# A mixture-of-experts kernel: the routing weights travel in the gathered rows, not in a table made by matmuls

## The chip, the cores and the metric

The kernel runs on one core of a Trainium2 chip. The metric is the device time of one execution in microseconds (us), lower is better; several executions are timed and the median is given. One further execution was taken by the hardware profiler.

## The reference

There are 2,048 tokens of 512 float32 values (4 batches of 512). The first stage multiplies each token by a dense matrix and adds a low-rank term chosen per batch; call its result `y`. The second stage is a mixture of 16 experts, of which each token uses two:

```
logits = y @ gate_w.T ; probs = softmax(logits)
topk_w, topk_idx = top_k(probs, 2) ; topk_w /= sum(topk_w) + 1e-20
g = y @ w_gate[e].T ; u = y @ w_up[e].T ; h = silu(g) * u      # 352 wide
out = x + sum over the two chosen e of topk_w * (h @ w_down[e].T)
```

## The kernel before, in words

The core has a matmul engine (TensorE, PE), two elementwise engines (VectorE, DVE, and ScalarE, ACT), GpSimd (POOL) and the engine that issues most transfers (SyncE, SP). Each runs its own list of instructions in order and waits on semaphores. `m_...` semaphores are counted up by PE, `v_...` by DVE, `a_...` by ACT, `d_...` by transfers. Every float32 product is made of three products of split values (high times high, high times low, low times high), so DVE and ACT split every operand into a high and a low part first.

**First stage.** `y` is made in 16 chunks `c` of 128 tokens: PE accumulates a chunk (`y_base`, `y_rank`), ACT copies it from its bank into `y_st` (`y_stage`), and SP stores it into the DRAM tensor `y_rows` (L395). In between, PE, ACT and DVE work out the routing: for each token its two experts, its softmax weights, and a slot for each of its two choices. Slots are sorted by expert and cut into tiles of 128 rows, all of one expert; a tile that an expert does not fill stays partly empty. There are 40 tiles in this run.

**The tables by slot.** A slot's token must be known by slot, but is computed by token. `slot_tables` (L607) does that with 32 small matmuls, one for each of the 32 pairs of chunk and choice: `oh_m` (one-hot of the place in a tile) times `oh_q` (one-hot of the tile, times the value to carry). `oh_q` has TABS = 5 values: two parts of the token's number, and the slot's weight cut into three bf16 parts (`w_part`). The first two tables are made in one pass of 32 matmuls during chunk 12 (`AT_TABLES`); the three weight tables in a second pass of 32 matmuls behind `gate_up(0)`. DVE makes the three weighted one-hots (`weigh`, L1090 and L1170), and adds up the three tables into `wtab` (L1177 to L1179). ACT scales a tile's result with its column of `wtab` in `y_weighted`.

**Second stage.** For each tile `t`, POOL gathers its 128 rows of `y_rows` into `xg` (`gather`, L1229). PE turns them over (`x_turn`, L625) for tiles below N_PE = 8. For the later ones SP copies them apart (`rows_apart`, L428) and DVE turns them (`x_turned`, L1150). ACT and DVE split the turned rows (`x_evac`, `y_low`), PE makes gate and up (`gate_up`, L693, 24 matmuls), ACT and DVE make `hh` (`silu`, L847, `product`, L1165), PE turns it (`h_turn`, L667) and makes the result (`down`, L722, 9 matmuls), ACT weighs it (`y_weighted`, L856), and POOL adds it to the output with an accumulating transfer (`scatter`, L1250). The order on each engine is written out by hand.

**The experts' weights.** An expert's weights come as two transfers, "gu" (1,408 KB) and "dn" (768 KB), into one of two raw buffers (`load_part`, L319), and ACT and DVE split them (L353, L355). The first expert's are loaded behind chunk 7's store. The second's are loaded behind chunk 15's store (`C_SECOND`). The third's are loaded by `later_weights(0)`, which SP comes to when gather 4 has landed (`N_LATE`). In this run tiles 0 to 2 belong to the first expert, 3 and 4 to the second, 5 to 7 to the third.

**The first gathers.** `gather(0)` and `gather(1)` may go before the last chunks are stored. PE turns the tokens' numbers of tiles 0 and 1 into one row (`need_turn`), DVE takes their maxima (`need`, semaphore `v_need`), and POOL waits for the stores up to these alone. `gather(2)` waits for all 16 stores, `gather(3)` for `h_turn(0)`, and `gather(4)` for `x_turn(2)`.

The lines that set this order at the beginning of the second stage, on PE:

```
gate_up(0)
e.wait_ge(v_ohq, 1)
e.wait_ge(v_need, 1)
slot_tables(bank[7], 2, TABS - 2)
words[1] = tile_word(e, 1)
h_turn(0)
gate_up(1)
x_turn(e, count, 2)
words[2] = tile_word(e, 2)
down(0)
```

Of the kernel before, what the change touches and what calls it, by code (L numbers as in the profile page):

```python
# [32 lines left out]
P = 128  # L33
# [34 lines left out]
TABS = 5  # L68
# [8 lines left out]
N_PE, NXS = 8, 4  # L77
N_LEAD, N_COPY = 9, 5
# [4 lines left out]
C_SECOND, N_LATE = CH - 1, 4  # L83
# [5 lines left out]
C_ID, C_IQ, C_TOK, C_ADP, C_AT, C_BEF, C_TOP, C_RNK, C_SEL, C_SCL, C_GT, C_IDS, CW = (  # L89
    0, P, P + TQ, *(P + TQ + CH + i for i in range(5)),  # L90
    *(P + TQ + CH + 4 + RANK + i for i in (0, P, P + 1, P + 1 + KH * NEXP, P + 1 + KH * NEXP + NBATCH)))
# [3 lines left out]
def build(nc, cst, rcst, head, head2, wt, wpt, wb, wbt, xin, x, wall, out):  # L95
    with ExitStack() as ctx:  # L96
# [7 lines left out]
        def region(start, size):  # L104
# [96 lines left out]
        late = [r_c(f"xg{i}", [P, H], F32) for i in range(N_EARLY, NXG)]  # L201
        ys = [r_c(f"ys{i}", [P, H], F32) for i in range(N_EARLY)]
        xg = [r_c(f"xg{i}", [P, H], F32) for i in range(N_EARLY)] + late
# [5 lines left out]
        w12 = r_c("w12", [P, NSEL], F32)  # L209
        w_part = [r_c(f"w_part{i}", [P, NSEL], BF16) for i in range(3)]  # L210
        w_rest = [r_c(f"w_rest{i}", [P, NSEL], F32) for i in range(2)]
        w_top = [r_c(f"w_top{i}", [P, CH], F32) for i in range(2)]
        w_sum, w_inv, w_one = [r_c(n, [P, CH], F32) for n in ("w_sum", "w_inv", "w_one")]
        tok_a, emp_f = [r_c(n, [P, TQ], F32) for n in ("tok_a", "emp_f")]
# [19 lines left out]
        y_dram = nc.dram_tensor("y_rows", [NTOK, H], F32, kind="Internal").ap()  # L234
# [19 lines left out]
        v_sh, v_cho, v_w12, v_ohq, v_ohm, v_tab, v_idx, v_w, v_gidx = [  # L254
            sem("v_" + n) for n in ("sh", "cho", "w12", "ohq", "ohm", "tab", "idx", "w", "gidx")]
# [59 lines left out]

        def load_part(e, part, ex, at):
# [42 lines left out]
        def _(e):  # L359
# [25 lines left out]
            for c in range(CH):  # L385
# [46 lines left out]
            for t in range(N_PE - N_COPY + 1):  # L432
                later_weights(t)
            for t in range(N_PE, NTILE + N_COPY):
                if t < NTILE:
                    rows_apart(t)
                if N_PE < t < NTILE - NRAW + N_COPY:
# [8 lines left out]
        def _(e):  # L446
# [169 lines left out]
            def x_turn(e, count, t):  # L616
                with in_use(e, count, t):
# [5 lines left out]
                    for k in range(KH):  # L623
                        rows = xg[t % NXG][:].rearrange("p (r k) -> p k r", k=KH)[:, k]
# [13 lines left out]
            for c in range(3, CH):  # L638
                for k in range(c == 3, KH):
# [112 lines left out]
        def _(e):  # L752
# [113 lines left out]
            split_weights(e, count, 3, ahead, "gu", a_gu)  # L866
            silu(1)
            x_evac(2)
# [31 lines left out]
        def _(e):  # L900
# [69 lines left out]
            done[0] += 4  # L970
# [37 lines left out]
            def token_weights():  # L1008
# [5 lines left out]
                e.tensor_tensor(w12[:, 0:CH], w1[:], w_one[:], ALU.mult).then_inc(v_chain, 1)  # L1014
                done[0] += 1
                step(e.tensor_tensor(w12[:, CH:NSEL], w2[:], w_one[:], ALU.mult))
                step(e.tensor_copy(w_part[0][:], w12[:]))
                step(e.tensor_tensor(w_rest[0][:], w12[:], w_part[0][:], ALU.subtract))
                step(e.tensor_copy(w_part[1][:], w_rest[0][:]))
                step(e.tensor_tensor(w_rest[1][:], w_rest[0][:], w_part[1][:], ALU.subtract))  # L1020
                e.tensor_copy(w_part[2][:], w_rest[1][:]).then_inc(v_w12, 1)
# [67 lines left out]
            def weigh(i):  # L1089
                e.tensor_tensor(oh_q[:, :, 2 + i], where, wide(w_part[i][:]), ALU.mult).then_inc(v_chain, 1)  # L1090
                done[0] += 1

            where = oh_q[:, :, 4]
# [3 lines left out]
            e.tensor_scalar(oh_q[:, :, 1], where, cs[:, C_AT:C_AT + 1], None, ALU.mult).then_inc(v_chain, 1)  # L1097
            done[0] += 1
            for k in range(TOPK):
                ks = slice(k * CH, (k + 1) * CH)  # L1100
                e.tensor_tensor(oh_q[:, ks, 0], where[:, ks], cs[:, C_TOK:C_TOK + CH].unsqueeze(2).to_broadcast([P, CH, TQ]),
                                ALU.mult).then_inc(v_chain, 1)
                done[0] += 1
            e.wait_ge(v_chain, done[0])
# [5 lines left out]
            step(e.tensor_scalar(tok_a[:], bank[4][:, 0:TQ], float(P), 0.0, ALU.subtract, ALU.max))  # L1110
            e.tensor_tensor(gidx[:], tok_a[:], bank[4][:, TQ:2 * TQ], ALU.add).then_inc(v_gidx, 1)
# [233 lines left out]
```

## Time and profile before

| | us |
|---|---|
| median of 3 executions | 348.83 (348.81 to 350.17) |
| the profiled execution, its own time | 347.8 |
| its span, first to last instruction | 346.0 |
| PE busy in the span | 335.8 (97%) |
| DVE busy | 233.8 (68%) |
| ACT busy | 179.0 (52%) |
| POOL busy | 129.7 (37%) |

The span is the stretch that the trace covers; 1.8 us of the execution's own time lie outside it. A busy share is an average over stages. What sets the end is read from the chain of work that ended last and from the idle time of the engine on it.

### The profile page before, as it was taken

How to read it: one execution, taken by the hardware profiler on the slowest of the kernel's cores; microseconds unless marked ns; L12 is line 12 of the kernel's file. 1: busy time of each engine (PE TensorE's matmuls, PEld its weight loads, DVE VectorE, ACT ScalarE, POOL GpSimd, SP SyncE). 2: the span in 40 equal slices, each digit the busy share in tenths (PEclk: the TensorE clock that was granted, in tenths of full speed). 3: DMA queues.
4: the chain of work that ended last, by engine and by line, in shares of the span. 5: the costliest groups of instructions: out<-in, count | busy, mean ns of one | idle time of the engine just before them, and what ended most of it. 6: DMA issues, size and time to landing. Idle time of an engine off the chain costs nothing.

```text
span 346.0 us, 7810 instructions
## 1 busy us (share of the span) xinstructions
PE 335.8 (97%) x1879; PEld 297.1 (86%) x1879; DVE 233.8 (68%) x307; ACT 179.0 (52%) x242; POOL 129.7 (37%) x85
## 2 busy tenths in 40 slices
PE   8999999999999899999999999999999999999992
PEld 4777878789899799899999999999999998989981
DVE  0586799988453558484878857788667588779320
ACT  1498711622546373655567554675545575575321
POOL 0000000023344461566284653757535271444323
PEclk9999999999999999999999999999999999999997
DMA  7991963847479899998999997899988969921153
GB/s 288 388 488 53 426 245 119 294 152 251 160 224 307 242 210 325 228 294 230 306 297 265 340 324 197 240 293 322 298 212 235 264 195 279 317 36 29 14 76 44
DMA packets 47352, 82.22 MB, mean 238 GB/s; under 512 B 5488, under 2 KB 22000, under 8 KB 47216
## 3 DMA queue, kind: packets, MB, share of 16 engines
q1 hardware_dynamic: 38336, 62.70, 54.9%
q0 software_dynamic: 8960, 18.89, 25.0%
q8 instruction: 22, 0.36, 0.4%
q14 instruction: 34, 0.28, 0.2%
HBM read 60.59 MB, written 19.92 MB: 233 GB/s over the span
## 4 chain that ended last, share of the span: by engine, by line
PE 91%; DMA 3%; DVE 2%; issue 1%; ACT 1%; POOLq 1%; DVEq 0%; ACTq 0%; POOL 0%
PE bank L693 43%; PE bank L722 23%; PE bank L449 4%; PE bank L667 4%; PE bank L549 4%; PE bank L553 4%; PE bank L550 4%; DMA xg<-y_rows,gidx 2%; PE bank L465 1%; PE bank L480 1%; PE bank L625 1%; PE bank L576 1%; DMA y_rows<-y_st 1%; POOLq L96 0%; DVE hh L1165 0%
## 5 line engine op out<-in xcount | busy, mean ns | idle before, releaser
L1250 POOL DMA_INDIRECT out<-ys,sidx x40 | 76.4, 1911 | 118.2 <-DMA out<-ys,sidx 71.0
L1229 POOL DMA_INDIRECT xg<-y_rows,gidx x40 | 52.7, 1319 | 94.4 <-issue 79.4
L693 PE MATMUL bank<-w_hi,xt_hi 128*128 x320 | 82.0, 333 | 0.3 <-issue 0.3
L355 DVE TENSOR_TENSOR w_lo<-w_raw,w_hi (+2 forms) x32 | 76.2, 2382 | 8.8 <-issue 5.9
L693 PE MATMUL bank<-w_hi,xt_lo 128*128 x320 | 79.0, 323 | 0.0
L693 PE MATMUL bank<-w_lo,xt_hi 128*128 x320 | 79.0, 323 | 0.0
L353 ACT ACTIVATE w_hi<-w_raw (+2 forms) x32 | 64.7, 2021 | 8.6 <-DMA w_raw<-wall 4.6
L847 ACT ACTIVATE sg<-bank 128x352 f32<-128x352 f32 x40 | 18.5, 462 | 75.6 <-PE bank L693 75.6
L693 PEld LDWEIGHTS bank<-w_lo,xt_hi 128*128 128x128 f32 x320 | 56.2, 189 | 0.0
L693 PEld LDWEIGHTS bank<-w_hi,xt_lo 128*128 128x128 f32 x320 | 56.1, 189 | 0.0
L693 PEld LDWEIGHTS bank<-w_hi,xt_hi 128*128 128x128 f32 x320 | 54.6, 189 | 1.4 <-issue 0.7
L1165 DVE TENSOR_TENSOR hh<-sg,bank 128x352 f32<-128x352 f32 x40 | 20.7, 518 | 46.0 <-ACT sg L847 46.0
L722 PE MATMUL bank<-w_hi,ht_hi 128*128 (+1 forms) x120 | 47.5, 395 | 0.1
L722 PE MATMUL bank<-w_lo,ht_hi 128*128 (+1 forms) x120 | 47.4, 395 | 0.0
L722 PE MATMUL bank<-w_hi,ht_lo 128*128 (+1 forms) x120 | 45.4, 400 | 0.0
L856 ACT ACTIVATE ys<-bank,wtab 128x512 f32<-128x512 f32 x40 | 27.4, 685 | 23.8 <-PE bank L722 23.8
L1150 DVE STREAM_TRANSPOSE xt<-xs 128x512 f32<-128x512 f32 x32 | 36.5, 1140 | 4.5 <-DMA xs<-xg 4.5
L1156 DVE TENSOR_TENSOR ht_lo<-bank,ht_hi 128x384 fp32r<-128x384 f32 x40 | 22.1, 553 | 19.2 <-ACT ht_hi L835 18.8
L722 PEld LDWEIGHTS bank<-w_hi,ht_hi 128*128 128x128 f32 (+1 forms) x120 | 22.6, 189 | 4.1 <-issue 0.6
L722 PEld LDWEIGHTS bank<-w_hi,ht_lo 128*128 128x128 f32 (+1 forms) x120 | 22.0, 188 | 4.5
L722 PEld LDWEIGHTS bank<-w_lo,ht_hi 128*128 128x128 f32 (+1 forms) x120 | 22.6, 188 | 3.6
L549 PE MATMUL bank<-w_base_hi,x_hi 128*128 128x512 f32 x64 | 25.6, 400 | 0.0
(181 smaller groups left out, 364.0 us busy)
## 6 DMA issues: line engine op xcount, KB each, us to landing
w_raw<-wall SPq DMA_DIRECT2D x16, 1408.0 KB, 8.0
w_raw<-wall SPq DMA_DIRECT2D x16, 768.0 KB, 9.8
xs<-xg SPq DMA_DIRECT2D x128, 64.0 KB
x_st<-xin SPq DMA_DIRECT2D x8, 512.0 KB, 13.3
y_rows<-y_st SPq DMA_DIRECT2D x16, 256.0 KB, 4.1
head_sb<-head SPq DMA_DIRECT2D x2, 640.0 KB, 5.1
wb_sb<-wb SPq DMA_DIRECT2D x2, 512.0 KB, 8.9
wbt_sb<-wbt SPq DMA_DIRECT2D x2, 512.0 KB, 10.8
```

The source lines that it names most:

```text
L353: e.activation(hi, raw, ACT.Copy).then_inc(own, 1)
L355: e.tensor_tensor(w_lo[:, bass.ds(dst, n)], raw, hi, ALU.subtract).then_inc(own, 1)
L549: e.matmul(dst, hi, w_base_hi[:, k], start=k == 0, stop=False, skip_group_check=True)
L693: mm = e.matmul(bank[2 + 2 * s + t % 2][:, 0:INTER], a, w[:, bass.ds(at + (k * GU + s * INTER), INTER)], start=k == 0 and i == 0, stop=k = ...
L722: mm = e.matmul(bank[6 + t % 2][:], a[t % 2][0:n, k * P:(k + 1) * P], w[0:n, bass.ds(at + (GUW + k * H), H)], start=j == 0, stop=j == 3 * ...
L847: e.activation(sg[t % 2][:], bank[2 + t % 2][:, 0:INTER], ACT.Silu).then_inc(a_sg, 1)
L856: e.activation(ys[t % NYS][:], bank[6 + t % 2][:], ACT.Copy, scale=wtab[:, t:t + 1]).then_inc(a_ys, 1)
L1150: e.transpose(xt[t % 2][:].rearrange("p (k i g) -> p g k i", k=KH, g=P // Q), xs[n % NXS][:].rearrange("p (g j k) -> p g k j", g=P // Q, k ...
L1156: e.tensor_tensor(ht_lo[t % 2][:], bank[1][:, 0:KI * P], ht_hi[t % 2][:], ALU.subtract).then_inc(v_ht, 1)
L1165: e.tensor_tensor(hh[t % 2][:], sg[t % 2][:], bank[4 + t % 2][:, 0:INTER], ALU.mult).then_inc(v_h, 1)
L1229: e.indirect_dma_start(out=xg[t % NXG][:], out_offset=None, in_=y_dram, in_offset=bass.IndirectOffsetOnAxis(ap=gidx[:, t:t + 1], axis=0)). ...
L1250: e.indirect_dma_start(out=out, out_offset=bass.IndirectOffsetOnAxis(ap=sidx[:, t:t + 1], axis=0), in_=ys[t % NYS][:], in_offset=None, bou ...
```

## The change

The two weights of a token are put into its row in DRAM, and a gather brings them with the row.

- `y_rows` gets rows of YW = 528 values (2,112 bytes) instead of 512 (2,048 bytes). The 16 values behind the 512 are the two weights and 14 zeros. They come from a new tile layout of `w12`, and one transfer, issued by SP ahead of chunk 12's store (`C_ROW`), writes them for all 2,048 tokens (2,048 pieces of 64 bytes). It waits for `v_w12`. `gather(0)` waits for it (`d_row`).
- DVE works out the token weights (`token_weights`) ahead of `sidx` and `need`, not behind them; the cut into three bf16 parts is gone.
- The three weight tables are gone: the second pass of 32 matmuls, three products on DVE, and the three additions. Instead DVE picks each tile's weight from the gathered row (`weigh(t)`, one instruction on 128x1 values), for every tile; `y_weighted(t)` and the reuse of a row buffer wait for it. To know whether a slot is its token's first or second choice, the token tables carry it (`at_a` up to 255, `is_top`).
- `gate_up(1)` follows `gate_up(0)` directly; `h_turn(0)` is in its middle.
- The second expert's weights are loaded behind chunk 13's store instead of chunk 15's. ACT's split of them waits for `m_y` (the last chunk) instead of the second table.
- `gather(3)` follows `gather(2)` directly; `gather(4)` waits for `h_turn(0)`. ACT does `x_evac(2)` ahead of `silu(1)`, DVE `y_low(2)` ahead of `product(1)`.
- N_PE is 7: tile 7 is copied apart by SP (four more transfers) and turned by DVE instead of PE.

```diff
-TABS = 5
+TABS, YW, W_PAD = 3, H + 16, 16
-N_PE, NXS = 8, 4
-N_LEAD, N_COPY = 9, 5
+N_PE, NXS = 7, 4
+N_LEAD, N_COPY, N_SOON = 9, 5, 4
-C_SECOND, N_LATE = CH - 1, 4
+C_SECOND, N_LATE, C_ROW = 13, 4, 12
...
-        y_dram = nc.dram_tensor("y_rows", [NTOK, H], F32, kind="Internal").ap()
+        y_dram = nc.dram_tensor("y_rows", [NTOK, YW], F32, kind="Internal").ap()
...
                     if t < NSPLIT:
-                        e.wait_ge(m_tb, 2)
+                        e.wait_ge(m_y, CH)
...
+                if c == C_ROW:
+                    e.wait_ge(v_w12, 1)
+                    e.dma_start(y_dram.rearrange("(c p) w -> p c w", p=P)[:, :, H:YW], w12[:]).then_inc(d_row, 16)
                 e.wait_ge(a_y, c + 1)
-                e.dma_start(y_dram[c * P:(c + 1) * P, :], y_st[c % NYST][:]).then_inc(d_y[c % NYST], 16)
+                e.dma_start(y_dram[c * P:(c + 1) * P, 0:H], y_st[c % NYST][:]).then_inc(d_y[c % NYST], 16)
                 if c == C_SECOND:
-                    e.wait_ge(v_w12, 1)
...
-            for t in range(N_PE - N_COPY + 1):
+            for t in range(N_SOON):
                 later_weights(t)
...
-                        if t == 2 and k == KH // 2:
+                        if t in (1, 2) and k == KH // 2:
                             h_turn(t - 1)
...
             gate_up(0)
-            e.wait_ge(v_ohq, 1)
-            e.wait_ge(v_need, 1)
-            slot_tables(bank[7], 2, TABS - 2)
-            words[1] = tile_word(e, 1)
-            h_turn(0)
             gate_up(1)
...
+            x_evac(2)
             silu(1)
-            x_evac(2)
...
+            token_weights()
             step(e.tensor_scalar(emp_f[:], bank[4][:, TQ:2 * TQ], 1.0, float(SKIP), ALU.is_lt, ALU.mult))
...
-            token_weights()
-            e.wait_ge(v_w12, 1)
-            weigh(0)
...
+            def weigh(t, done_by):
+                row = xg[t % NXG]
+                e.wait_ge(d_g[t % NXG], 16 * (t // NXG + 1))
+                e.scalar_tensor_tensor(wtab[:, t:t + 1], row[:, H:H + 1], is_top[:, t:t + 1], row[:, H + 1:H + 2],
+                                       ALU.mult, ALU.max).then_inc(done_by, 1)
...
             y_low(0)
-            weigh(1)
-            e.wait_ge(v_chain, done[0])
-            e.tensor_tensor(where, where, wide(w_part[2][:]), ALU.mult).then_inc(v_ohq, 1)
+            weigh(0, v_wt)
...
+            y_low(2)
+            weigh(2, v_wt)
             product(1)
-            y_low(2)
...
                 top = table(e, T_REX, T_NEED + t, C_FLOOR * P - 1, NTOK - 1)
+                if t == 0:
+                    e.wait_ge(d_row, 16)
...
             gather(2)
+            gather(3)
             e.wait_ge(m_ht, 1)
-            gather(3)
-            e.wait_ge(m_xt, 3)
             gather(4)
```

## Rows read from the trace of the kernel before

**Rows 1.** The page: busy us by engine, and the chain that ended last by engine.

```profile
PE 335.8 (97%) x1879; PEld 297.1 (86%) x1879; DVE 233.8 (68%) x307; ACT 179.0 (52%) x242; POOL 129.7 (37%) x85
...
PE 91%; DMA 3%; DVE 2%; issue 1%; ACT 1%; POOLq 1%; DVEq 0%; ACTq 0%; POOL 0%
```

**Rows 2.** Waits of PE, 76 to 346 us: for whom, total, times, longest.

```profile
PE bank L667 <- DVE hh L1165: 1.9, 2, 1.7
```

**Rows 3.** Timeline of PE: start, us, what, idle before and releaser.

```profile
82.98 2.17 PE L610 MATMUL bank<-oh_q,oh_m 128*128 128x144 bf16 x32
84.99 0.49 PE L667 MATMUL bank<-cs,hh 128*128 128x128 f32 x3
...
89.58 0.75 PE L625 MATMUL bank<-cs,xg 128*128 128x128 f32 x4 [0.23 <-DMA xg<-y_rows,gidx]
```

**Rows 4.** Timeline of PE, tiles 4 to 7.

```profile
114.41 0.55 PE L667 MATMUL bank<-cs,hh 128*128 128x128 f32 x3 [1.66 <-DVE hh L1165]
...
115.19 0.57 PE L693 MATMUL bank<-w_hi,xt_hi 128*128 x2
...
121.96 0.57 PE L693 MATMUL bank<-w_hi,xt_hi 128*128 x2
...
128.26 0.57 PE L693 MATMUL bank<-w_hi,xt_hi 128*128 x2
```

**Rows 5.** Timeline of ACT: the third expert's split.

```profile
106.01 2.56 ACT L353 ACTIVATE w_hi<-w_raw  x1 [2.05 <-DMA w_raw<-wall]
```

**Rows 6.** Timeline of DVE: the first and the last of six operations of `token_weights`.

```profile
68.48 0.16 DVE L1010 TENSOR_TENSOR w_top<-w_top,w_inv 128x16 f32<-128x16 f32 x1
...
69.47 0.17 DVE L1016 TENSOR_TENSOR w<-w_top,w_one 128x16 f32<-128x16 f32 x1
```

**Rows 7.** Timeline of POOL: gathers 0 and 4.

```profile
70.40 1.15 POOL L1229 DMA_INDIRECT xg<-y_rows,gidx  x1 [69.36 <-issue]
...
90.60 0.95 POOL L1229 DMA_INDIRECT xg<-y_rows,gidx  x1 [3.91 <-PE bank L625]
```

**Rows 8.** Timeline of PE: turning the rows of tiles 0 and 1.

```profile
75.97 0.63 PE L625 MATMUL bank<-cs,xg 128*128 128x128 f32 x4
...
80.56 0.63 PE L625 MATMUL bank<-cs,xg 128*128 128x128 f32 x4
```

**Rows 9.** Timelines of ACT (chunks 13, 15) and SP (loads); the chain's last store.

```profile
71.81 0.60 ACT L788 ACTIVATE y_st<-bank 128x512 f32<-128x512 f32 x1 [2.36 <-PE bank L576]
...
78.27 0.60 ACT L788 ACTIVATE y_st<-bank 128x512 f32<-128x512 f32 x1 [1.03 <-PE bank L576]
...
79.77 1.33 SPq L319 DMA_DIRECT2D w_raw<-wall  x2
...
78.90 1.98 DMA y_rows<-y_st
```

**Rows 10.** Queues: packets, MB, share of 16 engines; 70 to 72, 117.2 to 118, 341 to 343 us.

```profile
q1 hardware_dynamic: 144, 0.26, 34.7%
...
q1 hardware_dynamic: 136, 0.06, 26.9%
...
q0 software_dynamic: 131, 0.24, 88.0%
```

**Rows 11.** Transfers issued in 70.3 to 71 and 81 to 82 us: us to landing.

```profile
xg<-y_rows,gidx POOLq DMA_INDIRECT x1, 3.5
...
w_raw<-wall SPq DMA_DIRECT2D x1, 768.0 KB, 9.1
xg<-y_rows,gidx POOLq DMA_INDIRECT x1, 7.9
```

**Rows 12.** Stretches: length, busy of PE, PEld, DVE, ACT, POOL, PE clock, DMA share, GB/s.

```profile
115.00:330.00 215.00, 214.58 (x1230) 198.85 (x1229) 155.15 (x161) 120.02 (x161) 108.66 (x65) 1.00 0.87 238
...
342.00:343.00 1.00, 0.00 (x0) 0.00 (x0) 0.00 (x0) 0.00 (x0) 0.88 (x1) 0.74 0.94 172
```

**Rows 13.** Timeline of DVE: turning the rows of tile 8.

```profile
123.46 1.18 DVE L1150 STREAM_TRANSPOSE xt<-xs 128x512 f32<-128x512 f32 x1 [3.09 <-DMA xs<-xg]
```

More of the change, by code:

```diff
@@ L86 @@
 SKIP = 4096
[L89 to L91 removed]
+C_ID, C_IQ, C_TOK, C_ATK, C_ADP, C_AT, C_BEF, C_TOP, C_RNK, C_SEL, C_SCL, C_GT, C_IDS, CW = (
+    0, P, P + TQ, P + TQ + NSEL, *(P + TQ + NSEL + TOPK + i for i in range(5)),
+    *(P + TQ + NSEL + TOPK + 4 + RANK + i for i in (0, P, P + 1, P + 1 + KH * NEXP, P + 1 + KH * NEXP + NBATCH)))
 R_TRI, R_ONE, R_REV, R_THR, R_CUM, R_TH3, R_IM, RW = 0, P, 2 * P, 2 * P + 16, 2 * P + 32, 2 * P + 288, 2 * P + 293, 3 * P + 293
@@ L200, in build @@
         r_c = region(o_c, C_SIZE)
-        late = [r_c(f"xg{i}", [P, H], F32) for i in range(N_EARLY, NXG)]
+        late = [r_c(f"xg{i}", [P, YW], F32) for i in range(N_EARLY, NXG)]
         ys = [r_c(f"ys{i}", [P, H], F32) for i in range(N_EARLY)]
-        xg = [r_c(f"xg{i}", [P, H], F32) for i in range(N_EARLY)] + late
+        xg = [r_c(f"xg{i}", [P, YW], F32) for i in range(N_EARLY)] + late
         ys += [r_c(f"ys{i}", [P, H], F32) for i in range(N_EARLY, NYS)]
@@ L208, in build @@
         wtab = r_c("wtab", [P, TQ], F32)
-        w12 = r_c("w12", [P, NSEL], F32)
-        w_part = [r_c(f"w_part{i}", [P, NSEL], BF16) for i in range(3)]
-        w_rest = [r_c(f"w_rest{i}", [P, NSEL], F32) for i in range(2)]
+        w12 = r_c("w12", [P, CH, W_PAD], F32)
+        is_top = r_c("is_top", [P, TQ], F32)
         w_top = [r_c(f"w_top{i}", [P, CH], F32) for i in range(2)]
         w_sum, w_inv, w_one = [r_c(n, [P, CH], F32) for n in ("w_sum", "w_inv", "w_one")]
-        tok_a, emp_f = [r_c(n, [P, TQ], F32) for n in ("tok_a", "emp_f")]
+        at_a, emp_f = [r_c(n, [P, TQ], F32) for n in ("at_a", "emp_f")]
         gidx = r_c("gidx", [P, TQ], U32)
@@ L253, in build @@
             sem("v_" + n) for n in ("mask", "pick", "qpick", "qlo", "q", "mqg", "gpad", "glo")]
-        v_sh, v_cho, v_w12, v_ohq, v_ohm, v_tab, v_idx, v_w, v_gidx = [
-            sem("v_" + n) for n in ("sh", "cho", "w12", "ohq", "ohm", "tab", "idx", "w", "gidx")]
+        v_sh, v_cho, v_w12, v_ohm, v_tab, v_idx, v_wt, v_wx, v_gidx = [
+            sem("v_" + n) for n in ("sh", "cho", "w12", "ohm", "tab", "idx", "wt", "wx", "gidx")]
+        d_row = sem("d_row")
         v_zero, v_per = sem("v_zero"), sem("v_per")
@@ L1013, in token_weights @@
                 step(e.reciprocal(w_one[:], w_sum[:]))
[L1014 to L1021, printed above, removed]
+                step(e.tensor_tensor(w12[:, :, 0], w1[:], w_one[:], ALU.mult))
+                e.tensor_tensor(w12[:, :, 1], w2[:], w_one[:], ALU.mult).then_inc(v_w12, 1)
             e.wait_ge(m_rk, 1)
@@ L1087, in wide @@
                 return v.unsqueeze(2).to_broadcast([P, NSEL, TQ])
[L1089 to L1093, printed above, removed]
+            where = oh_q[:, :, 2]
             iqs = cs[:, C_IQ:C_IQ + TQ].unsqueeze(1).to_broadcast([P, NSEL, TQ])
@@ L1146, in x_turned @@
                 with in_use(e, count, t):
+                    weigh(t, v_wx)
                     e.wait_ge(d_xs[n % NXS], (n // NXS + 1) * 16 * (P // Q))
@@ L1174, in _ @@
             y_low(1)
+            weigh(1, v_wt)
             product(0)
-            e.wait_ge(m_tb, 2)
-            step(e.tensor_copy(wtab[:], bank[7][:, 2 * TQ:3 * TQ]))
-            step(e.tensor_tensor(wtab[:], wtab[:], bank[7][:, TQ:2 * TQ], ALU.add))
-            e.tensor_tensor(wtab[:], wtab[:], bank[7][:, 0:TQ], ALU.add).then_inc(v_w, 1)
             h_low(0)
@@ L1197, in _ @@
                         y_low(t + 1)
+                        weigh(t + 1, v_wt)
                     if N_PE <= t < NTILE:
@@ L1224, in gather @@
                     old = t - NXG
+                    if old >= 0:
+                        e.wait_ge(*weighed(old))
                     if 0 <= old < N_PE:
```

41 lines of the change are left out of this document (23 added, 18 removed).

## The prediction

> **What bounds the kernel now.** I read the page first: the chain that ended last is PE for 91% of the span, and PE is busy for 335.8 of 346.0 us [rows 1]. So an edit counts if it takes work off PE's list or removes a wait of PE, and it harms if it adds one; an edit on DVE, ACT, POOL or SP counts only through such a wait. Then I read PE's waits behind the first stage: they come to little more than 2 us, nearly all of it one wait of 1.66 us for `hh` ahead of `h_turn(4)` [rows 2, 4], and one of 0.23 us for gather 2 [rows 3]. From about 115 us on PE runs without a gap, one tile in 6.30 us (121.96 to 128.26) [rows 4]. The change can therefore gain only by what it takes from the stretch before 128 us, and by work that leaves PE. The last view is that of the queues and of the gathers around 70 to 90 us, since the new wait for the row transfer is there.
>
> **The change part by part.**
>
> *Second pass of the tables.* Its 32 matmuls start at 82.98 and the next instruction of PE starts at 84.99 [rows 3]: 2.01 us leave PE's list. Nothing hides them, PE waits neither ahead nor behind. Gain 2.01. `gate_up(1)` needs tile 1's rows split by 82.98 instead of 85.2: they are turned at 80.56 [rows 8], with 2.4 us left for one copy and one subtraction, and DVE has lost the products for the tables that stood in the way. No wait. `h_turn(0)` stands at about 85 either way.
>
> *Tile 7 off PE.* The tile with an `x_turn` ahead of it takes 115.19 to 121.96, 6.77 us, the next one without takes 6.30 [rows 4]: gain 0.47. On DVE it becomes a turn of 1.18 us like that of tile 8 [rows 13]; DVE is busy for 155 of the 215 us from 115 to 330 [rows 12], so it is hidden.
>
> *Gather 2.* PE waits 0.23 for it today [rows 3], as it took 7.9 us to land beside the second expert's loads, where gather 0, beside nothing, took 3.5 [rows 11]. The new order needs it at 89.58 - 0.23 - 2.01 = 87.3. Its issue waits for chunk 15's store, issued at 78.9 and landed in 1.98 [rows 9]. In the new order that store stands in SP's queue behind 2.2 MB of weights. They are issued 0.9 us behind chunk 13's copy (79.77 against 78.87 for chunk 15 [rows 9]), at 72.41 + 0.9 = 73.3 and 74.2; the later part took 9.1 us to land [rows 11], so 83.3, the store some 0.5 later, gather 2 at 84.2, landed at 87.7 with 3.5. Today's 0.23 goes, and a new wait of 0 (loads alone are quicker than beside a gather) to 1.6 us (landing in 4.7) comes. I take 0.6.
>
> *The third expert.* ACT waits 2.05 us for its weights at 106.01; DVE's split of the same weights is late by it, `product(4)` is queued behind that split, and PE waits 1.66 us for it [rows 4, 5]. SP issues this load when gather 4 has landed. Gather 4 now waits for `h_turn(0)` (85 [rows 3]) and for gather 3 to be issued, goes at about 87 and lands at 90.5 with 3.5; before it was issued at 90.60 [rows 7]. So the load can go 3.4 to 3.6 us sooner. PE's list moves up by the 2.2 above less 1.1 of new waits below, so ACT's wait shrinks by at least 2.3, more than its 2.05, and PE's 1.66 behind it goes; without new waits it shrinks by 1.2, and up to 0.85 of it could stay. Gain 1.66.
>
> *DVE's list.* 40 `weigh` of about 0.2 us (the 128x16 operations take 0.16 to 0.17 [rows 6]) are 8 us more over the run, against the products, cuts and additions saved; they stand behind a `y_low` whose rows have landed, so none waits. Hidden by DVE's 60 idle us [rows 12]. If that cover were gone each would cost 0.2. The tokens' one-hots cost the same as before to 0.1 us. Rows of 2,112 instead of 2,048 bytes are 3% more for 40 gathers, which are issued tiles ahead: nothing.
>
> *The row transfer: the term that decides.* `v_w12` now comes 1.2 us behind `toks`: the six operations take 68.48 to 69.64 [rows 6] and start at about 67.4, so SP can issue at 68.7. `need` comes behind them and `is_top`, 1.35 later, which moves gather 0 from 70.40 to 71.75 at the earliest [rows 7]. Its rows are needed at 75.97 [rows 8]; 71.75 + 3.5 = 75.3, so the old slack of 2.1 us carries this. The transfer has 2,048 runs of 64 bytes, 128 for each of 16 engines. No row shows such a write. Store packets of 2,048 bytes: 34.7% of 16 x 2 us over 144 = 77 ns; packets of 512 bytes: 26.9% of 16 x 0.8 us over 136 = 25 ns [rows 10]. A line through both gives 8 ns for none and 10 ns for 64 bytes. Bounds: 8 ns, and 77 ns, as if each were a full store. Beside it stand about 1.3 us: a store of 8 packets for each engine, 0.6 us, lands in 1.98 [rows 9]. So it lands at 68.7 + 1.3 + 128 x 10 ns = 71.3, ahead of 71.75, at 10 ns; at 77 ns it is 79.9. I take 10 ns, since the two measured sizes lie on a line towards it and queue and source are the same.
>
> The limit is narrow. Chunks 12 and 13 and then the weights (73.3) follow in the same queue; a gather issued later than about 72.3 meets the weights and lands in up to 7.9 instead of 3.5. That is reached when a run costs 15 to 18 ns. *The Trainium skill, DMA: Bandwidth & Descriptors, Specifications, says that below 512 B a transfer does a read-modify-write. No row here has such a store; the rule's result is the second rival below.*
>
> Gather 1 follows at about 73.2, just beside the weights: landed at 76.7 to 81.1, needed at 80.56 [rows 8]: 0 to 0.6, I take 0.4. At x_turn(0) I take 0.1. Behind them, tile 8's rows: DVE waits 3.09 us for them at 123.46 without PE waiting [rows 13]. PE is there over 4 us sooner and the transfers some 3 to 5; 0 to 1.5, I take 0.2.
>
> **Sum.** -2.01 - 0.23 - 0.47 - 1.66 = -4.37; new waits 0.1 + 0.4 + 0.6 + 0.2 = +1.3; together -3.1. The profiled execution's own time is 347.8 (span 346.0 and 1.8 around it), which gives 344.7. The median of the runs is 1.0 above it, so 345.7.
>
> **Rivals.**
>
> 1. *The waits come back elsewhere (within 0.5%).* Gather 2, needed 2.2 us sooner, stands behind a store that stands behind 2.2 MB; gather 1 runs beside them; tile 8's rows hang on scatters that serialize. With the upper bounds, 0.6 + 1.6 + 1.5 + 0.1 = 3.8, the net is -0.6, or 348.2. For it speaks that gather 2 took 7.9 us beside loads [rows 11]; against it that all transfers of the stage are issued sooner too.
>
> 2. *The row transfer is slow (slower).* If a 64-byte run is read and written, its price is like that of the accumulating scatter, which reads and writes: 88.0% of 16 x 2 us over 131 is 215 ns against 77 for the store [rows 10], 2.8 times; 10 ns become 28, the transfer lands at 73.6, gather 0 goes at 74.0 beside the weights and lands at up to 81.9, 5.9 us behind 75.97. The four gains remain, gathers 1 and 2 are then no extra wait: 5.9 - 4.4 = +1.5. Behind it stands the clock: with PE idle, as it is at the end, the granted clock is 0.74 in 342 to 343, so on its way from 2.4 to 1.2 GHz [rows 12]; an idle stretch of 5.9 us would meet that, and each us at that level costs half a us; I allow 0 to 2. So 350.3 to 352.3. It decides from about 16 ns on: a wait of 4.4 us, where the gain is gone, needs gather 0 to land at 80.4. At 77 ns it is 79.9 + 0.4 + 7.9 - 76.0 = 12.2, a net of +7.8, 356.6. For it: nothing of this size has been measured, and the margin is 0.8 us. Against it: the line of rows 10. *Worked out by the skill's rule alone, the time is this rival's: 350.3 instead of 345.7.*
>
> 3. *No new wait.* All bounds at zero: -4.4, 344.4.
>
> **How the numbers follow.** Forecast (-3.1, with its own range of 344.9 to 347.0) 0.48; no new wait 0.12; waits come back 0.17; row transfer slow 0.23. A change of 0.5% (1.7 us: below 347.1 or above 350.6) is about what a measurement of this kernel can tell from none. The first two are faster: 0.60. The waits that come back are within it, and so is the mild end of the slow transfer (0.04): 0.21. The rest of it is slower: 0.19. Range 343.7 (no new wait and 0.7 for terms that I have at nothing) to 351.0 (the slow transfer at its mild end with half of the clock's price); it leaves out the heavy end of the slow transfer.
>
> **What would show it.** Right: no L610 behind 80 us; PE's waits without L667 <- DVE; `gate_up(2)` starts near 91.6 instead of 92.7; ACT doesn't wait for `w_raw` ahead of the third expert's split; the row transfer lands below 3 us from its issue and gather 0 is issued before 72.3. Wrong: a wait of several us of PE at L625 around 76 us with a releaser `xg<-y_rows`, and gather 0 released by the row transfer; then the price of 64-byte runs is the step that failed. A wait at L625 near 87 us with gather 2 behind it is rival 1; a PE clock below 1.00 between 76 and 90 is the clock's part of rival 2.

## The result, and the profile after

| | before | after |
|---|---|---|
| median of the runs, us | 349.12 (347.65 to 352.39, 12 runs) | 352.56 (351.16 to 354.96, 12 runs) |
| profiled execution: its own time, span | 347.8, 346.0 | 352.81, 350.9 |

The ratio is 1.0104, with a 95% interval of 1.008 to 1.0127. The change made the kernel 1% slower. I had forecast 345.7 us and a range up to 351.0: the sign and the range are both wrong. Ratios, here and below, are of executions in the chip's undisturbed state; two of the four of `e7_apart_tile7_split_later` were in a slower one, its profiled execution among them.

The profiled executions are 4.9 us apart in their spans, the medians 3.4. The kernel before was profiled in a quick execution, 1.3 us below its median, the kernel after in one at its median. So the stretches below overstate the loss by some 1.5 us, which no trace here places.

The page of the kernel after, busy us and the chain that ended last. Against [rows 1], PE lost 36 matmuls and still is busy for 0.6 us more, and its share of the chain fell from 91% to 74%:

```profile
PE 336.4 (96%) x1843; PEld 296.6 (85%) x1843; DVE 232.6 (66%) x339; ACT 179.4 (51%) x242; POOL 130.0 (37%) x85
...
PE 74%; DVE 9%; DMA 9%; issue 3%; POOL 2%; SPq 1%; ACT 1%; DVEq 0%; ACTq 0%; POOLq 0%
```

The waits of PE behind 60 us (for whom, total, times, longest). [Rows 2] had one line of weight, 1.9 for `hh`; now that is 0.4 and three others have come:

```profile
PE bank L631 <- DMA xg<-y_rows,gidx: 3.9, 1, 3.9
PE bank L729 <- DVE ht_lo L1154: 1.2, 1, 1.2
PE bank L631 <- DVE xt_lo L1133: 1.1, 1, 1.1
PE bank L674 <- DVE hh L1163: 0.4, 1, 0.4
```

The same waits in the timeline of PE (start, us, what, idle before and releaser). The first row answers to [rows 8]: `x_turn(0)` at 80.51 instead of 75.97. The second is the first instruction of `gate_up(1)`:

```profile
80.51 1.13 PE L631 MATMUL bank<-cs,xg 128*128 128x128 f32 x4 [3.92 <-DMA xg<-y_rows,gidx]
...
89.80 0.58 PE L700 MATMUL bank<-w_hi,xt_hi 128*128 x2
...
97.92 0.72 PE L631 MATMUL bank<-cs,xg 128*128 128x128 f32 x4 [1.08 <-DVE xt_lo L1133]
...
124.33 0.49 PE L729 MATMUL bank<-w_hi,ht_hi 128*128 x1 [1.21 <-DVE ht_lo L1154]
```

**Where the 4.9 us came from.** The starts of `down(t)` in PE's timelines, before and after, and in two kernels of the experiments (`e2_second_at_15` and `e9_loads_parted`, below):

| tile t | 0 | 1 | 2 | 3 | 4 | 5 | 6 |
|---|---|---|---|---|---|---|---|
| before | 90.15 | 97.02 | 103.77 | 110.52 | 119.16 | 125.92 | 132.22 |
| after | 94.50 | 102.68 | 109.46 | 116.24 | 124.33 | 130.73 | 137.01 |
| after less before | 4.35 | 5.66 | 5.69 | 5.72 | 5.17 | 4.81 | 4.79 |
| e2 | 91.03 | 97.91 | 104.67 | 111.45 | 120.94 | 128.91 | 135.21 |
| e9 | 91.06 | 97.92 | 104.68 | 111.46 | 118.18 | 124.94 | 131.21 |

Up to `down(0)`: `x_turn(0)` is 4.54 late: 3.92 is the wait, and PE came 0.62 later to it, of which 0.36 was there by 29 us and 0.40 by 69. From there to the end of `gate_up(0)` it takes 89.80 - 80.51 = 9.29 us, where it was 82.98 - 75.97 = 7.01 [rows 3, 8]: 2.28 more. The second pass of the tables is gone, -2.01. From `gate_up(1)` or `h_turn(0)` to `down(0)` it is 4.70 instead of 5.16, -0.46, with the 0.23 of gather 2 in it. The sum is +4.35. `xt_lo` adds 1.31 at tile 1, the third expert's weights give 0.55 back at tile 4 and tile 7's missing turn 0.36 at tile 5. Behind it nothing changes.

The 2.28 us are the clock's (it costs 2.55, and 0.27 of idle time that this stretch had before is gone). Stretches of the kernel after: length, busy of PE, PE clock, DMA share, GB/s. The granted clock was 1.00 through this stretch before; here it falls while PE idles, stays at 0.50, the lower of its two levels (1.2 GHz of 2.4), up to 86 us, and is whole again from 87:

```profile
79.00:80.00 1.00, 0.00 (x0) 0.83 1.04 417
...
80.00:86.00 6.00, 5.49 (x17) 0.50 0.55 204
87.00:88.00 1.00, 1.00 (x9) 1.00 0.00 0
```

**Why gather 0 is late.** The chain of the kernel after, in order of time (start, us, what):

```profile
69.18 2.99 DMA y_rows<-w
72.17 0.02 issue
72.19 0.10 POOLq L1258
...
72.58 0.07 POOLq L1258
72.65 0.05 issue
72.70 0.02 POOLq L1259
72.72 0.66 issue
73.38 0.23 POOLq L299
73.61 6.86 DMA xg<-y_rows,gidx
```

The row transfer lands at 72.17. POOL then goes through four waits for stores, a semaphore, 0.66 us in which it waits for nothing that the profile shows, and a register instruction, and issues gather 0 at 73.61, 1.44 us later; [rows 7] had 70.40. The gather then takes 6.86 us to land and not 3.5 [rows 11], as SP has issued the second expert's weights at 73.73 (timeline of SP: start, us, what); that the weights are the cause is shown by `e2_second_at_15` below. The second row of POOL's timeline is gather 2:

```profile
73.73 1.32 SPq L323 DMA_DIRECT2D w_raw<-wall  x2
```

```profile
73.61 1.15 POOL L1226 DMA_INDIRECT xg<-y_rows,gidx  x1 [72.58 <-DMA y_rows<-y_st]
...
88.11 0.94 POOL L1226 DMA_INDIRECT xg<-y_rows,gidx  x1 [12.06 <-DMA y_rows<-y_st]
```

The queues of the kernel after (packets, MB, share of 16 engines). The first row is 70.5 to 71 us, in which only the row transfer's 64-byte packets run: 91.7% of 16 x 0.5 us over 875 packets is 8.4 ns for one. The other two are 74 to 78 us and 78 to 80: in the first four microseconds beside the weights the gather (q0) moves nothing, so its queue isn't listed.

```profile
q1 hardware_dynamic: 875, 0.06, 91.7%
...
q1 hardware_dynamic: 435, 1.12, 88.3%
...
q1 hardware_dynamic: 179, 0.47, 59.2%
q0 software_dynamic: 102, 0.37, 45.0%
```

In the trace the gather's first packet is at 78.38, 4.8 us behind its issue. Before, it was at 72.26, 1.9 us behind 70.40.

**The other two waits.** Timeline of ACT: `x_evac(2)`, the copy of tile 2's turned rows (L800, 96.47), starts when a split of 2.56 us ends; the rows were turned at 94.11. `xt_lo` and `x_turn(3)` hang on it.

```profile
94.01 2.56 ACT L357 ACTIVATE w_hi<-w_raw  x1 [1.15 <-issue]
96.47 0.57 ACT L800 ACTIVATE xt_hi<-bank 128x512 fp32r<-128x512 f32 x1
```

Timeline of DVE: the turn of tile 7, new on DVE, waits for its copied rows, and the split and `h_low(4)` (the low part of tile 4's `hh`) are queued behind it. `down(4)` at 124.33 waits for the last row:

```profile
120.90 1.14 DVE L1148 STREAM_TRANSPOSE xt<-xs 128x512 f32<-128x512 f32 x1 [2.54 <-DMA xs<-xg]
121.90 1.72 DVE L359 TENSOR_TENSOR w_lo<-w_raw,w_hi  x1
123.54 0.55 DVE L1154 TENSOR_TENSOR ht_lo<-bank,ht_hi 128x384 fp32r<-128x384 f32 x1
```

### The profile page after: what moved, and what is told of

Read it like the earlier page. It is cut to its first block, busy times and chain, and to the rows that moved or that the text cites. A ratio compares the mean times of both kernels' runs of the same rounds, so it can differ in the third digit from the quotient of the medians.

```text
span 350.9 us, 7809 instructions
## 1 busy us (share of the span) xinstructions
PE 336.4 (96%) x1843; PEld 296.6 (85%) x1843; DVE 232.6 (66%) x339; ACT 179.4 (51%) x242; POOL 130.0 (37%) x85
## 4 chain that ended last, share of the span: by engine, by line
PE 74%; DVE 9%; DMA 9%; issue 3%; POOL 2%; SPq 1%; ACT 1%; DVEq 0%; ACTq 0%; POOLq 0%
PE bank L700 40%; PE bank L729 21%; DMA xg<-y_rows,gidx 4%; PE bank L674 3%; PE bank L455 3%; DMA xs<-xg 2%; DMA head_sb<-head 2%; POOL out L1247 2%; DVE oh_m L1097 1%; PE bank L555 1%; PE bank L559 1%; PE bank L556 1%; PE bank L486 1%; DMA y_rows<-w 1%; SPq L434 1%
## 5 line engine op out<-in xcount | busy, mean ns | idle before, releaser
L1247 POOL DMA_INDIRECT out<-ys,sidx x40 | 81.2, 2031 | 119.1 <-DMA xs<-xg 38.5
L1226 POOL DMA_INDIRECT xg<-y_rows,gidx x40 | 48.3, 1207 | 98.2 <-DMA y_rows<-y_st 84.9
L1148 DVE STREAM_TRANSPOSE xt<-xs 128x512 f32<-128x512 f32 x33 | 37.5, 1136 | 3.6 <-DMA xs<-xg 3.6
```

What stands on the lines that cost most here:

```text
L1148: e.transpose(xt[t % 2][:].rearrange("p (k i g) -> p g k i", k=KH, g=P // Q), xs[n % NXS][:].rearrange("p (g j k) -> p g k j", g=P // Q, k ...
L1226: e.indirect_dma_start(out=xg[t % NXG][:], out_offset=None, in_=y_dram, in_offset=bass.IndirectOffsetOnAxis(ap=gidx[:, t:t + 1], axis=0)). ...
L1247: e.indirect_dma_start(out=out, out_offset=bass.IndirectOffsetOnAxis(ap=sidx[:, t:t + 1], axis=0), in_=ys[t % NYS][:], in_offset=None, bou ...
```

## The experiments

The theory was: gather 0 is late by the work of POOL between the landing and the issue, and so falls beside the weights. The rivals: it is late by the loads alone, whenever it is issued about there; and the loss is tile 7's or ACT's order, not the gather's.

**e1_row_wait_last.** The wait for the row transfer stands last, so that the four waits for stores go through while the transfer runs.

```diff
-                if t == 0:
-                    e.wait_ge(d_row, 16)
                 stores = [...]
                 for i in range(NYST):
                     e.wait_ge(d_y[i], stores[i])
+                if t == 0:
+                    e.wait_ge(d_row, 16)
```

> The changed kernel, with gather 0's wait for the row transfer moved behind the reading of the stores it needs and the waits for them. Theory (the gather is late by POOL's own steps between the landing of the row transfer, 72.17, and the issue, 73.61, and so meets the second expert's loads): gather 0 is issued at about 72.3, lands by 76.5, PE's wait of 3.92 us at the first turning goes nearly all, so does the half clock behind it (2.1 us): span about 345, some 5.5 us below the changed kernel and 1% below the kernel before. Rival (the loads delay any gather whose packets are not done when they start, at about 75): issue 72.3, landing still 79 to 80, PE's wait 2.6 to 3.6 us, and a time 1 us below the changed kernel or less.

Measured: 352.94 us, ratio 1.0101 (1.0049 to 1.0154). Gather 0 was issued 3.90 us behind the row transfer's issue (69.94, 73.84) instead of 4.43, and PE still waited 4.1 us at `x_turn(0)`. Of the 1.44 us only 0.5 could be taken out in this way: 0.92 are left between the landing (72.92) and the issue. So gather 0 was not issued at 72.3, as the theory had it; it went 0.6 us ahead of the loads (74.45), and the rival's wait came.

**e2_second_at_15.** `C_SECOND = CH - 1`: the second expert's weights behind chunk 15's store, as in the kernel before.

> The changed kernel with the second expert's loads behind chunk 15's store, as before the change. Theory (the loads ahead of gather 0 are what holds it for 6.86 instead of 3.5 us): gather 0 issued at 73.6 lands at 77.1, PE waits 0.7 us instead of 3.92 and keeps its clock; but gather 2 stands beside the loads again and PE, which needs it 2 us sooner than before, waits some 2 us for it: about 1 us below the kernel before, 4 us below the changed one. Rival (the row transfer itself, or rows of 2,112 bytes, make gathers slow): landing still 6 us or more behind the issue, and no gain on the changed kernel.

Measured: 350.8 us, 1.0054 (1.0024 to 1.0084). Gather 0 was issued at 73.79, later than in the change, and landed in 3.52. Timeline of PE: `x_turn(0)` waits 0.57, the clock is kept, and `down(0)` starts at 91.03. So it is the loads that hold the gather. In the table above, its row is 0.9 behind the kernel before up to `down(3)`. The rest of the time went to tile 7's chain, at `down(4)`, and to the clock, which fell to 0.50 behind that wait (`down(4)` to `down(5)` is 7.97 us, against 6.40 in the change):

```profile
77.36 0.75 PE L631 MATMUL bank<-cs,xg 128*128 128x128 f32 x4 [0.57 <-DMA xg<-y_rows,gidx]
...
120.94 0.49 PE L729 MATMUL bank<-w_hi,ht_hi 128*128 x1 [2.53 <-DVE ht_lo L1154]
```

Gather 2, issued at 83.61 beside the loads, made PE wait 1.5 us. The theory's gain on the kernel before did not come: it had left tile 7's chain out.

**e3_tile7_on_pe.** `N_PE = 8`: tile 7 is turned by PE again, all else as in the change.

> The changed kernel with N_PE = 8 again, so that PE turns tile 7's rows. Theory (DVE, waiting 2.5 us for tile 7's copied rows, is late with tile 4's low part, for which PE waits 1.2 us): PE's wait for ht_lo goes, and PE does 0.47 us more: 0.7 us below the changed kernel. Rival (what PE waited for is the third expert's weights, as before): the wait turns up as one for hh, and the time is 0.5 us above the changed kernel.

Measured: 352.19 us, 1.0085 (1.0049 to 1.0121). The wait for `ht_lo` is gone, as the theory says; the three others stay (4.6, 1.1, 0.4). The time is 0.4 us below the change's, where 0.7 was expected; the two intervals overlap, so the gain in time is not shown.

**e4_wait_last_tile7.** Both edits, those of e1 and e3.

> Both edits: the row wait last, and N_PE = 8. Theory: the gains add up, 6.2 us below the changed kernel, 2.8 below the kernel before. Rival: with PE 5.5 us sooner the third expert's loads come too late again, and PE waits 1 to 2 us for hh at tile 4: 1 to 2 us below the kernel before.

Measured: 351.67 us, 1.008 (1.0059 to 1.0101). Gather 0 was issued at 73.17, 0.6 us ahead of the loads (73.80), and landed in 7.5 all the same; its first packet ran at 78.42. To be issued ahead of the loads is not enough: undisturbed, the first packet comes 1.9 us behind the issue (72.26 against 70.40 before, 75.63 against 73.79 in e2), and the loads, with packets from 74.9 on, come in between. Neither the theory (2.8 us below the kernel before) nor its rival came: this time is 0.9 us below the change's, with overlapping intervals. The kernel before, timed beside e1 to e4, gave 349.2 us.

**e5_weights_apart.** The weights get a DRAM tensor of their own and a gather of their own, so that gather 0 doesn't wait for them. Short form:

```diff
+        w_dram = nc.dram_tensor("w_rows", [NTOK, W_PAD], F32, kind="Internal").ap()
...
-                if t == 0:
-                    e.wait_ge(d_row, 16)
...
             gather(1)
+            e.wait_ge(d_row, 16)
+            for t in range(N_EARLY):
+                gather_w(t)
```

Later tiles issue `gather_w(t)` behind their `gather(t)`, `need` comes ahead of `token_weights` again, the row transfer goes behind chunk 12's store (`C_ROW = 13`), and DVE's `weigh(0)` and `weigh(1)` go behind `product(0)`.

> The changed kernel, but the weights lie in a DRAM tensor of their own (2,048 rows of 64 bytes) and each tile has a second, small gather for them; gathers 0 and 1 no longer wait for the row transfer, DVE makes need ahead of the token weights, as before the change, and the row transfer goes behind chunk 12's store. Theory (gather 0 is late by the row transfer and what POOL does behind it, and so lands beside the loads): gather 0 is issued at 70.8 and lands by 74.5, PE has no wait at 76 and keeps its clock; that gives back 3.9 and 2.1 us, less 0 to 1 for the small gathers: 5 to 6 us below the changed kernel, 1.5 to 2.5 below the kernel before. Rival (the loads behind chunk 13 catch the first gathers anyway): PE still waits at the turning of tile 0 or 1 for several us, and the time is that of the changed kernel within 1 us.

Measured: 356.81 us against 348.51, 1.0217 (1.0154 to 1.0281). The first half came as expected: gather 0 at 71.04, no wait at `x_turn(0)`, the clock at 1.00 up to 124 us. But everything behind it got worse. Chunk 15's store is in SP's queue behind 2.2 MB of weights; the chain:

```profile
79.44 7.66 DMA y_rows<-y_st
```

It took 1.98 us before [rows 9]. Gather 2 went at 87.86 and PE waited 1.78 us for it, 5.0 us in three pieces for `hh` (the first, of 1.97, already at 87.7) and 4.9 at `down(4)`. So loads behind chunk 13's store collide with gather 0, or, when that goes in time, with the last store and through it with gather 2. How much of the loss is the loads' and how much the doubled gathers' was not parted.

**e6_apart_tile7** and **e7_apart_tile7_split_later.** e5 with `N_PE = 8`; e7 also puts ACT's `x_evac(2)` and `silu(1)` ahead of the split of the second expert's gate and up.

> As the one before, and PE turns tile 7 (N_PE = 8). Theory: PE's wait for ht_lo at tile 4 (1.2 to 2.5 us in the runs so far) goes and 0.47 us comes: 1 to 2 us below the one before. Rival: the wait was for the third expert's weights, which come no sooner: a wait for hh of the same size, no gain.

> As the one before, and ACT splits tile 3's weights behind x_evac(2) and silu(1), not ahead. Theory (PE waits 1.08 us at x_turn(3) since x_evac(2) is queued behind that split of 2.56 us): the wait of 1.08 goes, nothing else moves: 1 us below. Rival (ACT's list is full there): the wait moves to hh or ht_lo of tile 1 or 2, no gain.

Measured: e6 359.01 us, 1.0287 (1.0229 to 1.0345); e7 353.78 and 358.66 us, 1.0228 (1.0134 to 1.0321). Neither gain came; both are as slow as e5 within the intervals. In e6 the wait for `ht_lo` fell from 4.9 to 2.5 us and that for `hh` grew from 5.0 to 8.2, in five pieces: the rival. Why `hh` comes late there was not followed to its end.

**e8_before_tile7_dve.** The kernel before with `N_PE = 7` and nothing else: tile 7 on DVE by itself.

> The kernel before with this one edit: tile 7 turned by DVE (N_PE = 7, SP's order of later loads kept). Forecast's step: 0.47 us less, hidden on DVE. Theory from the changed kernel: DVE waits for tile 7's copied rows ahead of the low part of tile 4, PE gets a wait for ht_lo of 1 to 2.5 us instead of some of its 1.66: 0 to 1.5 us slower than the kernel before.

Measured: 350.22 us, 1.0077 (1.0044 to 1.0109). Timelines of DVE and PE:

```profile
118.34 1.14 DVE L1150 STREAM_TRANSPOSE xt<-xs 128x512 f32<-128x512 f32 x1 [4.31 <-DMA xs<-xg]
```

```profile
121.80 0.49 PE L722 MATMUL bank<-w_hi,ht_hi 128*128 x1 [2.88 <-DVE ht_lo L1156]
```

This edit alone makes the kernel slower. PE's wait hangs on a chain of DVE: 4.31 us of waiting for the copies, the turn of 1.14, a split, `h_low(4)`. Neither the waiting nor the turn is hidden.

**e9_loads_parted.** From e4, and the second expert's loads are parted: gate and up (1,408 KB) behind chunk 14's store, down (768 KB) behind chunk 15's.

```diff
-                if c == C_SECOND:
-                    for part in PARTS:
+                if c in (CH - 2, CH - 1):
+                    for part in (("gu",) if c == CH - 2 else ("dn",)):
```

> The changed kernel with the row wait last, PE turning tile 7 (N_PE = 8), and the second expert's two loads parted: gu behind chunk 14's store, dn behind chunk 15's. Theory (every large load ahead of the first two gathers or of the last store costs PE, behind them it costs nothing): gathers 0 and 1 land in 3.5 us, PE waits 0.5 us at 76, the clock stays; chunk 15's store waits for gu alone and lands near 83, gather 2 near 88: no wait or 0.5. The 2.0 us of the tables stay gained and 1 us of the wait for the third expert: 345 to 347, 0.5 to 1.3% below the kernel before. Rival (the gain of the tables is always given back, since gather 2 needs the last store and its rows are wanted 2 us sooner): a wait of 1.5 to 2.5 us at x_turn(2), and the time of the kernel before within 0.5%.

Measured: 346.94 us against 348.59, 0.9941 (0.9918 to 0.9963): faster than both kernels. The first load goes at 76.86, with gather 0's packets nearly through (the last ends at 77.2), and its own packets run from 78.8 on. The chain:

```profile
69.38 2.97 DMA y_rows<-w
...
73.29 3.97 DMA xg<-y_rows,gidx
77.26 0.04 issue
77.31 0.75 PE bank L631 x4
...
80.83 4.84 DMA y_rows<-y_st
...
86.44 4.01 DMA xg<-y_rows,gidx
```

`x_turn(0)` waits 0.55 us and `x_turn(2)` 1.56, the clock is 1.00 throughout; the waits for `xt_lo` and `ht_lo` are gone and that for `hh` is 0.3. In the table above, the row is 0.9 behind the kernel before at `down(0)` and 1.0 ahead from `down(4)` on: the second pass and the third expert's wait are gained, two gathers are paid. (0.55 us of lag was there by 29 us.)

The time is as expected, gather 2's wait is not: up to 0.5 us was allowed for it, and 1.56 is the rival's. And the table shows that parting the loads is not what gained: the rows of e2, with both loads behind chunk 15's store, and of e9 are the same to 0.03 us up to `down(3)`. They part at `down(4)`, where e2 has tile 7's chain and e9 has not. A kernel with the loads left behind chunk 15 and tile 7 on PE was not run; by these rows it could be as fast as e9.

**e10_loads_parted_late3.** e9 with `N_LATE = 3`: the third expert's load behind gather 3.

> As the one before, and the third expert's loads wait for gather 3 instead of gather 4. Theory: they are issued 2 to 3 us sooner, what is left of PE's wait at tile 4 goes (0.5 to 1.5 us). Rival: they meet gather 4 and 5 and the first scatter, and PE waits at a later turning: no gain or a loss up to 2 us.

Measured: 346.77 us, 0.9951 (0.9925 to 0.9977), the same as e9. Gather 2 made no wait (it was issued at 85.00, 1.4 us sooner than in e9), but the wait for `xt_lo` ahead of `x_turn(3)`, 1.1 us, was back. In e9 the two lie on top of each other: 2.1 us for both gathers, here 0.5 and 1.1. The 1.4 us are not the edit's, which changes nothing ahead of gather 3's landing (90.57): chunk 15's store took 3.39 us to land here and 4.84 in e9. By so much do two executions differ in this stretch.

**e11_both_loads_at_14.** e4 with both loads behind chunk 14's store.

> As e9, but both loads behind chunk 14's store. Theory: the first gathers are as free as in e9 (PE's wait at 76 about 0.5), but chunk 15's store stands behind 2.2 MB and lands at 85 or later instead of 83, and gather 2 with it: PE waits 1 to 2 us more at x_turn(2) than in e9. Rival (a store is not held by loads ahead of it in the same queue): same wait as in e9, within 0.3 us.

Measured: 351.37 us, 1.0066 (1.0031 to 1.01). Up to `down(7)` its profile is that of e9 to 0.3 us: gather 2 makes the same wait, 1.56 us, and chunk 15's store took 5.36 us instead of 4.84, so the theory failed there and the rival held. In the profile two waits of PE come later: 1.1 at 144.9 us, behind copies of rows that took 10.7 us to land, and 1.2 at 236.6, behind a split that waited 2.7 us for an expert's weights. They make up nearly all of the 2.6 us between the two spans (347.7 and 345.1). But the profiled execution (349.58) is 1.8 below its median. Five of the ten executions, of 351.85 to 353.25 us, have a mean granted clock of 0.984 to 0.987, the profiled one 0.997; those of e9 lie between 0.993 and 0.998. So most of them lost clock at a place that no trace here shows. How the place of one load near 80 us brings all this is open.

**e12_parted_late3_act_order.** e10 with ACT's `x_evac(2)` and `silu(1)` ahead of the split.

> The loads parted as in e9_loads_parted, the third expert's load behind gather 3 as in e10_loads_parted_late3, and on ACT the order x_evac(2), silu(1), and then the split of the second expert's gate and up (tile 3's), not that split first. Theory: the wait of 1.08 us of PE for xt_lo ahead of x_turn(3) is ACT's queue: x_evac(2) stands behind a split of 2.56 us. With the order turned round that wait is below 0.3, and the split ends about 1.1 us later, which gate_up(3) has to spare, so the time is about 1 us below that of e10_loads_parted_late3: about 345.8, a ratio of 0.992. Rival: the split is then late for DVE, whose part of the same weights and product(1) stand behind it; the same 1 us comes back as a wait for w_hi, w_lo or hh, and the ratio stays at 0.995.

Measured: 348.05 us against 349.06, 0.9967 (0.9941 to 0.9994): no better than e10. The rival holds. Timeline of DVE, then of PE:

```profile
95.02 3.09 DVE L359 TENSOR_TENSOR w_lo<-w_raw,w_hi  x1 [2.44 <-ACT w_hi L357]
```

```profile
98.86 0.49 PE L729 MATMUL bank<-w_hi,ht_hi 128*128 x1 [1.77 <-DVE ht_lo L1154]
```

DVE's split waits for ACT's, `h_low(1)` is queued behind it, and PE waits 1.77 us for that. In the profiled execution, which is 1.2 us above the median, the clock then falls (stretches as above):

```profile
97.00:99.00 2.00, 0.23 (x2) 1.00 1.04 409
99.00:101.00 2.00, 2.00 (x7) 0.66 0.92 175
101.00:103.00 2.00, 2.00 (x8) 0.50 0.96 253
```

The wait for `xt_lo` only went from 1.1 to 0.7. So ACT's order as it stands in the change is at least as good.

## Why the prediction was wrong, by its steps

**The step that failed is the sentence that sets the margin of the row transfer:** it lands at 71.3, "ahead of 71.75", and gather 0 goes at 71.75, below the limit of 72.3. Two of its terms were short:

- The landing. Issue 68.7 was 69.18 (of the 0.48 late, 0.40 is the lag that was there by 69 us), and 1.3 + 1.28 = 2.6 us was 2.99: the runs of 64 bytes took 1.1 and what stands beside them 1.9. So 72.17.
- From the landing to the issue I had nothing. It is 1.44 us, and 0.9 with the wait put last (e1). The chain of the kernel before could have told this, where chunk 15's store lands at 80.88 [rows 9] and gather 2, which waits for it, is issued 0.76 us later:

```profile
80.94 0.70 issue
81.64 7.90 DMA xg<-y_rows,gidx
```

This is the larger error, and it was enough by itself: a landing at 71.3 and 1.44 us give 72.7, behind the limit of 72.3.

Together gather 0 went at 73.61 and not at 71.75. That there is such a limit was right: gathers 0 issued at 73.17 and 73.61 with the loads at 73.7 to 73.8 landed in 7.5 and 6.9 us (e4, after), with the loads moved away in 3.5 to 4.0 (e2, e9), and with an issue at 71.04 and 71.56 in 4.9 (e5, e6). No run issued one between 71.6 and 73.1, so 72.3 itself is untested.

**The second rival had the result, for the wrong reason.** It gave 350.3 to 352.3, with a wait of 5.9 us and up to 2 for the clock; measured were 352.56, 3.9 and 2.3. Its cause was a price of 16 ns or more for a run of 64 bytes. The runs took 8.4 ns, my line's 10 ns was on the safe side, and the transfer's own packets were through in 1.4 us (70.12 to 71.51). I had tied the case to that price alone, and so gave it 0.23, where the margin of 0.55 us had two more terms: the landing's and POOL's. My sign for a slow transfer (a wait at L625 with gather 0 behind the row transfer) came as well, and would have named the wrong step.

*The Trainium skill, DMA: Bandwidth & Descriptors, Specifications, gives 512 B as the least size of a transfer for the full rate, and says that a smaller one is read, modified and written. The first half agrees: 64 bytes in 8.4 ns are 7.6 bytes per ns, against 26.6 for 2,048 in 77 [rows 10]. For the second half the page has no price, and 8.4 ns for a packet, below the 25 ns of a 512-byte store, shows none; for this transfer the measurement decides.*

**Second pass of the tables:** right, -2.01, and `gate_up(1)` follows without a wait.

**Tile 7 off PE:** the sign was wrong. The tile on PE is shorter by 0.36, near my 0.47, but the turn on DVE has to wait for its copies (2.54 in the change, 4.31 in e8), and PE waits 1.2 and 2.9 us for what is queued behind it. I called it hidden by DVE's 60 idle us [rows 12], an average over 215 us. At this place the copies come late twice over. SP issues them when gather 7 has landed (110.96 in the change), and they take 9.9 us to land, beside the fourth expert's loads, issued at 105.00 and 108.17. Timeline of SP (the third expert's loads are the first two of the four):

```profile
98.27 10.29 SPq L323 DMA_DIRECT2D w_raw<-wall  x4
110.98 13.05 SPq L434 DMA_DIRECT2D xs<-xg  x12
```

I had read [rows 13], where tile 8's turn waits 3.09 us; the same wait one tile sooner was the thing to price. In the change PE was late itself, which hid 1.3 us of it against e2.

**Gather 2:** in the change nothing, since PE comes 4.5 us late; there chunk 15's store went at 85.29, behind the weights, and landed in 2.05. Where PE is in time it made waits of 1.56 us (e9) and of none (e10, the same code up to there), on either side of the 0.6 that I took. That the store lands 0.5 behind the load ahead of it was near: 0.7 in e9 (84.97, 85.66) and 1.3 in e5 (85.81, 87.10). The terms for gather 1 and tile 8's rows, 0.4 and 0.2, came to nothing in the change and in e9.

**Third expert:** the mechanism was right. ACT's split of it waits for no transfer, and the wait for `hh` went from 1.66 to 0.4. In the change 1.2 us was lost again at the same tile to tile 7's chain; in e9 `down(4)` comes 6.72 us behind `down(3)`, where it was 8.64, a gain of 1.92.

**Missing from the sum:** 1.08 us for `xt_lo` at `x_turn(3)`. I had looked at DVE's list for tile 2 and not at ACT's, where the split is in the queue. With gather 2 and PE sooner, `x_evac(2)` falls behind it.

**`weigh` and wider rows:** right; 0.2 us each, hidden.

In e9 three of the four gains (tile 7 stays on PE) and the new waits stand side by side: ratio 0.9941, or 2.0 us of 348.59, where the forecast without tile 7's 0.47 would be 2.6. The change lost through the place of the second expert's loads (e2), and through tile 7 (e8, and the rows of e2 against e9).

## What to carry to other kernels

Where a step fits by less than a microsecond, list every instruction between the release and the issue, also those of a queue that seem to cost nothing, and give each term that no row covers a chance of its own, instead of tying the margin to one cause. A transfer moved up is paid for by the small transfers behind and beside it: here 2.2 MB moved up by two chunks cost a wait of 3.92 us and 2.5 of clock, and left where they were (e2) they cost 0.57 there, no clock, and 1.5 at gather 2. A change made of several parts is best run part by part: parting the loads looked like the cure, and the table shows that its share in it is unproven. Hiding work on another engine by its average idle time says nothing about what it waits for at that place: look at the next instance of the same work in the trace.

## What the runs showed of the hardware

- **A gather beside a large load is held, not slowed.** Issued 0.1 and 0.6 us ahead of 2.2 MB from SP, its first packet ran 4.8 and 5.3 us behind its issue instead of 1.9, and then the whole gather was through in 1.5 us, against 1.3 alone. In the packets of the traces it starts as those of the first load (1,408 KB) run out: at 78.38 where their last ends at 80.1 (after), at 87.10 with 85.8 for gather 2 of the kernel before, and at 87.79 with 87.6 for that of e2, the last two issued 1.9 us behind the load. *The Trainium skill, DMA: Bandwidth & Descriptors, Issuing engines are not separate DMA queues, says that transfers of different engines interleave on the same 16 DMA engines. From 78 us on they do, at 45% and 59% of the engines; in the four microseconds ahead the rows show no packet of the gather.* Why it stands behind the first load and runs beside the second was not found.
- **64-byte packets from a store are cheap:** 8.4 ns each, and 2,048 of them landed in 2.99 us, 1.9 of which is beside the packets' own time.
- **The clock is lost after some waits and not after others.** It fell to 0.50 behind waits of PE of 3.92 (after), 2.53 (e2), 4.87 (e5) and 1.77 us (e12), and stayed at 1.00 behind 2.88 (e8), 1.66 (before) and 1.56 us (e9). The cost was 2.5 us in the change. The length of the wait alone doesn't order these. Each is one profiled execution, and others of the same kernel can differ: of e8's seven, the profiled one is the quickest with a mean clock of 0.997, and three of 352 us have 0.992 to 0.994.
- **POOL needs 0.8 to 0.9 us from its last wait to the issue of an indirect transfer:** for gather 0 0.9 (0.66 without a releaser and 0.23 for a register instruction), in the change and in e1 and e9 alike; for gather 2 0.8 (80.88 to 81.64 before, 85.66 to 86.44 in e9). What fills the 0.66 the profile does not show.
